# Attention and a mixture of experts on one core: joined normalisations, copies moved to ScalarE, and an earlier merge of the two output sums

## The reference, cut to what matters

```
x = x + xattn(layernorm(x), ctx, mask)      # x: 16 batches x 112 tokens x 512
x = x + ffn(layernorm(x), ...)

xattn:  scores = q @ m.T / sqrt(512), masked; softmax over 375; readout = attn @ m
ffn:    probs = softmax(x @ gate.T)            # 1792 tokens, 64 experts
        top 8 of each token, weights normalised to sum 1
        experts that are only second choices (rank 5 to 8 of every token that has them) and are
        similar enough to a first choice are replaced by it
        y = down_e(silu(gate_e(x)) * up_e(x))   # 192 inner columns
        out[token] += weight * y
layernorm(x) = (x - mean) / sqrt(var + 1e-5)    # no scale, no shift
```

## Time and profile before

| | |
|---|---|
| median of three runs | 810.89 us |
| profiled execution | 809.93 us, its span 808.1 us |
| PE, busy share of the span | 84% |
| DVE | 69% |
| POOL | 64% |
| ACT | 56% |
| mean granted clock of TensorE | 0.934 of full speed |
| memory traffic | 190 MB, mean 235 GB/s |

### The profile page before, as it was taken

One profiled execution on the slowest core, in us unless ns is written; L12 is line 12 of the kernel. 1 busy time (PEld: TensorE's weight loads), 2 busy tenths in 40 slices (PEclk: granted clock), 3 DMA queues, 4 the chain that ended last, 5 costly groups with the idle time before them and its releaser, 6 DMA issues. The chain is left out here.

```text
span 808.1 us, 15268 instructions
## 1 busy us (share of the span) xinstructions
PE 678.4 (84%) x4278; PEld 560.5 (69%) x4278; DVE 554.3 (69%) x1308; ACT 453.6 (56%) x885; POOL 518.3 (64%) x461
## 2 busy tenths in 40 slices
PE   4999999731599999999999998989898998999730
PEld 2555555420489999888988888878787887888630
DVE  5699999962277666777677677676767776767620
ACT  3544554210266666666775766767666676666620
POOL 6037777776638887887766666676657666666440
PEclk9999999955599999999999999999999999999965
DMA  8999896605659999999999999999999999999467
GB/s 281 373 369 336 292 312 232 206 18 161 171 153 221 241 234 242 237 239 257 244 270 254 272 243 245 258 234 260 241 252 222 252 236 240 237 248 242 92 124 159
DMA packets 107557, 189.93 MB, mean 235 GB/s; under 512 B 33521, under 2 KB 35441, under 8 KB 106065
## 3 DMA queue, kind: packets, MB, share of 16 engines
q1 hardware_dynamic: 74274, 125.61, 50.7%
q0 software_dynamic: 33200, 63.35, 38.1%
HBM read 143.40 MB, written 56.24 MB: 247 GB/s over the span
## 5 line engine op out<-in xcount | busy, mean ns | idle before, releaser
L1224 PE MATMUL bank<-xh,w1h 128*128 128x256 f32 (+7 forms) x768 | 228.8, 298 | 18.3 <-DVE h L897 18.2
L1226 PE MATMUL bank<-xh,w1l 128*128 128x256 f32 (+7 forms) x768 | 220.4, 287 | 0.0
L1225 PE MATMUL bank<-xl,w1h 128*128 128x256 f32 (+7 forms) x768 | 220.4, 287 | 0.0
L610 POOL DMA_INDIRECT xg<-normed_tokens,list x145 | 158.2, 1091 | 54.1 <-issue 48.2
L1224 PEld LDWEIGHTS bank<-xh,w1h 128*128 128x128 f32 x768 | 147.2, 192 | 23.4 <-issue 23.2
L619 POOL DMA_INDIRECT out_rows<-ys,list x73 | 115.8, 1587 | 70.9 <-ACT ys L1041 58.1
L594 POOL DMA_INDIRECT list_table<-token,slot x112 | 114.4, 1022 | 69.8 <-DVE token L765 36.6
L619 POOL DMA_INDIRECT second_sum<-ys,list x70 | 113.3, 1618 | 66.4 <-ACT ys L1041 45.5
L913 DVE TENSOR_TENSOR xl<-bank,xh 128x448 fp32r<-128x448 f32 (+3 forms) x145 | 84.2, 616 | 97.3 <-ACT xh L1048 96.3
L1225 PEld LDWEIGHTS bank<-xl,w1h 128*128 128x128 f32 x768 | 147.7, 192 | 0.0
L1226 PEld LDWEIGHTS bank<-xh,w1l 128*128 128x128 f32 x768 | 147.5, 192 | 0.0
(11 more groups left out here) (210 smaller groups left out, 1104.4 us busy)
## 6 DMA issues: line engine op xcount, KB each, us to landing
raw<-in_w SPq DMA_DIRECT2D x195, 256.0 KB, 4.7
raw<-in_w2a SPq DMA_DIRECT2D x65, 256.0 KB, 4.5
ctxT_s<-in_ctxT SPq DMA_DIRECT2D x16, 768.0 KB, 8.4
ctx_s<-in_ctx SPq DMA_DIRECT2D x16, 768.0 KB, 8.1
raw<-in_w2b SPq DMA_DIRECT2D x65, 128.0 KB, 5.8
list_table<-blank SPq DMA_DIRECT2D x30, 256.0 KB, 6.7
x_in<-in_x SPq DMA_DIRECT2D x16, 224.0 KB, 7.9
out_rows<-x SPq DMA_DIRECT2D x16, 224.0 KB, 6.6
```

The lines of the kernel that those rows point to most:

```text
L610: pool.indirect_dma_start(xg[u.on(XGS)][0:u.m, t, :], None, normed, bass.IndirectOffsetOnAxis(ap=lists[u.on(LISTS)][0:u.m, t, 0:1], axis=0 ...
L1224: pe.matmul(bank[m][:, 0:W], wh, mh, start=(c == 0), stop=False)
L1225: pe.matmul(bank[m][:, 0:W], wh, ml, start=False, stop=False)
L1226: mm = pe.matmul(bank[m][:, 0:W], wl, mh, start=False, stop=(c == DK - 1))
```

## The change

1. The two normalisations share their tiles, two columns wide, and one chain `scales(s)` on VectorE: column 0 is the x of batch s+1, column 1 the x1 of batch s-2. Statistics of x are made one slot earlier (lag -2), x is loaded one slot earlier (lag -4), and the pipeline has one more slot in front, -4, that only loads. `newton` works on two columns at once.
2. `publish` moves to ScalarE, at the end of its slot; VectorE keeps the counting of token numbers (`count_tokens`), with a semaphore of its own, `c_token`, for which POOL waits as well.
3. The merge is issued before the late loop, when all static scatters have landed; `scatter_over` waits for it and adds to `out`.

```diff
         def phase1(eng, body):
-            for n in range(-3, B + 5):
+            for n in range(-4, B + 5):
                 body(At(n))
...
-                batches(s, (-3, load_x), (-2, load_ctxT), (-1, load_ctx))
+                batches(s, (-4, load_x), (-2, load_ctxT), (-1, load_ctx))
...
+                split_wait(pool, c_token, (b.n + 1) * TOKEN)
                 split_wait(pool, c_slots, (b.n + 1) * SLOTS)
...
                 split_wait(pool, ys_s, u.t0 + 1)
-                pool.indirect_dma_start(second, bass.IndirectOffsetOnAxis(ap=over_list[:], axis=0),
+                pool.wait_ge(merged, 16)
+                pool.indirect_dma_start(out, bass.IndirectOffsetOnAxis(ap=over_list[:], axis=0),
...
+            for i in range(2):
+                pool.wait_ge(scattered[i], SUM_TILES[i] * 16)
+            pool.dma_start(out[0:TOK, :], second[0:TOK, :], accum_op=ALU.add, max_dma_last_dim=8192).then_inc(merged, 16)
             overs = overs_of(pool)
             with pool.Fori(0, overs) as g:
                 keep_list(Unit(STATIC, g))
                 gather(Unit(STATIC, g + 1))
                 scatter_over(Unit(STATIC, g))
-            pool.wait_ge(scattered[0], SUM_TILES[0] * 16)
-            split_wait(pool, scattered[1], (overs + SUM_TILES[1]) * 16)
-            pool.dma_start(out[0:TOK, :], second[0:TOK, :], accum_op=ALU.add, max_dma_last_dim=8192).then_inc(merged, 16)
...
+            def scales(s):
+                if not -1 <= s.n < B + 2:
+                    return
+                ch = Chain(dve, c_scale, SCALED, s.n + 1)
+                dve.wait_ge(c_norm, min(s.n + 2, B) * NORM)
+                wait(dve, c_resid, min(max(s.n - 1, 0), B) * RESID)
+                yield from ch.link(v.tensor_scalar(rstd["var"][:], mv[s.n % 2][:, :, 1], EPS, None, ALU.add), tell=True)
+                dve.wait_ge(rough_s, (s.n + 2) * 2)
+                yield from ch.link(v.tensor_tensor(rstd["square"][:], rstd["rough"][:], rstd["rough"][:], ALU.mult))
+                yield from ch.link(v.scalar_tensor_tensor(rstd["half"][:], rstd["square"][:], -0.5, rstd["var"][:], ALU.mult, ALU.mult))
+                wait(dve, xn_s, min(s.n + 1, B))
+                wait(dve, xn2_s, min(max(s.n - 2, 0), B))
+                yield from ch.link(v.scalar_tensor_tensor(rstd["exact"][:], rstd["half"][:], 1.5, rstd["rough"][:], ALU.add, ALU.mult))
+                yield from ch.link(v.scalar_tensor_tensor(rstd["shift"][:], mv[s.n % 2][:, :, 0], -1.0, rstd["exact"][:], ALU.mult, ALU.mult), tell=True)
+                ch.done()
...
-                yield from ch.link(v.tensor_scalar(slot8[b.four][:], bank[7][:, 0:ENTERS], -1.0, float(PAD_LIST), ALU.mult, ALU.add))
-                yield from ch.link(v.tensor_copy(token[b.four][:, :, 1].bitcast(F32), bank[7][:, ENTERS:2 * ENTERS]))
                 yield from ch.link(v.tensor_scalar(token[b.four][:, :, 0], token[b.four][:, :, 0], 4 * T, None, ALU.add), tell=True)
...
-                    taking_turns(s, (4, place_entries), (3, top), (-1, norm_and_scale), (2, renormed_x))
+                    going = [scales(s)]
+                    batches(s, (4, lambda b: going.append(place_entries(b))), (3, lambda b: going.append(top(b))),
+                            (-2, lambda b: going.append(norm(b))))
+                    turns(*going)
                 taking_turns(s, (0, score))
                 if s.n == 0:
                     constants()
                 taking_turns(s, (1, resid))
-                taking_turns(s, (4, publish))
+                taking_turns(s, (4, count_tokens))
...
+            for i in range(2):
+                v.memset(mv[i][:], 1.0).then_inc(primed, 1)
+            dve.wait_ge(primed, 2)
             phase1(dve, slot)
...
+            def rough(s):
+                if -1 <= s.n < B + 2:
+                    act.wait_ge(c_scale, (s.n + 1) * SCALED + 1)
+                    a.activation(rstd["log"][:], rstd["var"][:], ACT.Ln).then_inc(rough_s, 1)
+                    act.wait_ge(rough_s, (s.n + 1) * 2 + 1)
+                    a.activation(rstd["rough"][:], rstd["log"][:], ACT.Exp, scale=-0.5).then_inc(rough_s, 1)
+            def publish(b):
+                act.wait_ge(spread_ps, b.n + 1)
+                wait(act, tabled[b.four], b.turn4 * ENTERS * 16)
+                a.activation(slot8[b.four][:], bank[7][:, 0:ENTERS], ACT.Copy, scale=-1.0, bias=float(PAD_LIST))
+                a.copy(token[b.four][:, :, 1].bitcast(F32), bank[7][:, ENTERS:2 * ENTERS]).then_inc(c_slots, SLOTS)
...
-            phase1(act, lambda s: batches(s, (1, copy_pT), (-1, rough(rough_a, c_norm, NORM, rstd_a)), (2, norm_x1),
-                                          (3, exps), (-1, norm_x), (2, copy_xn2T), (0, exp_scores), (-1, copy_xnT),
-                                          (1, rough(rough_c, c_resid, RESID, rstd_c))))
+            def slot(s):
+                batches(s, (1, copy_pT))
+                rough(s)
+                batches(s, (2, norm_x1), (3, exps), (-1, norm_x), (2, copy_xn2T), (0, exp_scores), (-1, copy_xnT), (4, publish))
```

More of the change, by code:

```diff
@@ L164, in two1 @@
             return [sb1(f"{name}{i}", shape, dt) for i in range(2)]
-        def rstd_tiles(name):
-            return {k: early.enter_context(nc.sbuf_tensor(f"rstd_{name}_{k}", [T, 1], F32)) for k in ("var", "log", "rough", "square", "half", "exact")}
         def sem(name):
@@ L239, in program @@
         mask_s = sb1("mask_s", [B, M], U8); masked = sb1("masked", [B, M], BF16); of_batch = sb1("of_batch", [B, B, T], BF16)
-        st_a = sb1("st_a", [T, 6]); mv_a = sb1("mv_a", [T, 2]); rstd_a = rstd_tiles("a")
+        st_a = sb1("st_a", [T, 6]); mv = two1("mv", [T, 2, 2])
+        rstd = {k: sb1(f"rstd_{k}", [T, 2]) for k in ("var", "log", "rough", "square", "half", "exact", "shift")}
         xn = two1("xn", [T, D])
         xnT = two1("xnT", [P, DK, T])
-        shift_a = sb1("shift_a", [T, 1]); shift_c = sb1("shift_c", [T, 1])
         nmax = two1("nmax", [T, 1])
@@ L249, in program @@
         rinv = sb1("rinv", [T, 1]); rval = sb1("rval", [T, 1])
-        st_c = sb1("st_c", [T, 6]); mv_c = sb1("mv_c", [T, 2]); rstd_c = rstd_tiles("c")
+        st_c = sb1("st_c", [T, 6])
         xn2T = two1("xn2T", [P, DK, T])
@@ L660, in norm @@
                 dve.wait_ge(x_in[b.on(XS)], (b.nth(XS) + 1) * 16)
-                wait(dve, xn_s, b.n)
                 yield from ch.link(v.bn_stats(st_a[:], xa[b.on(XS)][:]))
-                yield from ch.link(v.bn_aggr(mv_a[:], st_a[:]))
-                yield from ch.link(v.tensor_scalar(rstd_a["var"][:], mv_a[:, 1:2], EPS, None, ALU.add), tell=True)
+                yield from ch.link(v.bn_aggr(mv[(b.n + 1) % 2][:, 0, :], st_a[:]), tell=True)
                 ch.done()
[L667 to L671, removed]
@@ L678, in normed_x @@
                 ch.done()
-            def norm_and_scale(b):
-                yield from norm(b)
-                yield from normed_x(b)
             def score(b):
@@ L704, in resid @@
                 yield from ch.link(v.bn_stats(st_c[:], x1[b.on(STORED)][:]))
-                yield from ch.link(v.bn_aggr(mv_c[:], st_c[:]))
-                yield from ch.link(v.tensor_scalar(rstd_c["var"][:], mv_c[:, 1:2], EPS, None, ALU.add), tell=True)
-                ch.done()
-            def renormed_x(b):
-                ch = Chain(dve, c_renorm, RENORM, b.n)
-                dve.wait_ge(rough_c, (b.n + 1) * 2)
-                wait(dve, xn2_s, b.n)
-                yield from newton(ch, rstd_c)
-                yield from ch.link(v.tensor_scalar(shift_c[:], mv_c[:, 0:1], -1.0, rstd_c["exact"][:], ALU.mult, ALU.mult), tell=True)
+                yield from ch.link(v.bn_aggr(mv[b.n % 2][:, 1, :], st_c[:]), tell=True)
                 ch.done()
@@ L996, in copy_xnT @@
                 a.activation(xnT[b.par][:], bank[0][:, 0:DK * T].rearrange("p (c t) -> p c t", c=DK), ACT.Copy, scale=SCALE).then_inc(xnT_sb, 1)
-            def rough(s, c, links, r):
-                def stage(b):
-                    act.wait_ge(c, (b.n + 1) * links)
-                    a.activation(r["log"][:], r["var"][:], ACT.Ln).then_inc(s, 1)
-                    act.wait_ge(s, b.n * 2 + 1)
-                    a.activation(r["rough"][:], r["log"][:], ACT.Exp, scale=-0.5).then_inc(s, 1)
-                return stage
+            def rough(s):
[9 more added lines that the diff above has]
+                a.copy(token[b.four][:, :, 1].bitcast(F32), bank[7][:, ENTERS:2 * ENTERS]).then_inc(c_slots, SLOTS)
             nc.scalar.preload_act_table_set("natural_log_exp_and_others")
```

25 lines of the change are left out of this document (10 added, 15 removed).

## The result

The changed kernel takes 805.14 us (median of 5 runs, 803.35 to 807.05), the kernel before beside it 812.53 us (median of 5 runs, the three known before among them): ratio 0.9924, 95% interval 0.9899 to 0.9949. (The ratio on record isn't the quotient of these two medians, which would be 0.9909.) In a second measurement it gave 0.994 (0.9928 to 0.9952), 805.5 against 810.88 us, while a copy of the kernel before gave 1.0013 (0.9997 to 1.0029). It is faster by 0.6 to 0.8%, some 5 to 6 us. I had forecast 812.3 us and a range down to 808.0: wrong in sign and outside the range.

What follows compares the result with a forecast made beforehand. POOL's 112 list scatters were taken to bound routing, and one chain through the merge the end. Routing +0.2 and merge +1.2 us on the median 810.89 gave 812.3 us, range 808.0 to 815.0.

Steps and rivals of the forecast that it cites:

- Start and first token: Ahead of the first list scatter: start +0.4 us, ScalarE's publish -0.2 us, PE's waits unchanged; routing together +0.2 us.
- rival 4: Routing stage: PE and ScalarE wait on the joined root, POOL starves and loses 3 us, 815 us in all; chance 0.13.
- Take 0; bounds -3 and +3: Routing stage: list scatters lengthened beside VectorE's products, 5.8 us in all, stay as they are since the same products stay.
- rival 3: Routing stage: freed VectorE shortens it, -9 us (some 803); small form, collisions halved, -3 us (809); chance 0.10.
- So 796.2 + 3.7 + 0.6 = 800.5: End: merge's landing alone at 796.2, plus 3.7 us for loads and 0.6 for the gather inside it; end +1.2 us.
- rival 1: End: loads slip into the merge's gaps and cost it little; tail -3.1 us, 808.0 in all; chance 0.20.
- Rival 2: End: the speculative unit's gather stands behind the merge on q0 and its chain ends the program, +2 to +3 us; chance 0.15.
- Sum: Whole kernel: routing +0.2 and merge +1.2 us give +1.4 us, so 812.3 us on the scale of the medians.

Runs made afterwards that it cites:

- a_again: The changed kernel measured once more, unchanged, against the kernel before: ratio 0.994, 805.5 against 810.88 us.
- after_wait: The changed kernel with one more wait on GpSimd, already satisfied, ahead of the late scatter: 841.44 us, a single run.
- gather_late: The changed kernel with the late loop's gather issued behind the late scatter instead of ahead of it: ratio 0.9981 to the kernel before.
- weights_late: The changed kernel with SyncE's late weight loads held back until the merge has landed: ratio 0.996 to the kernel before, against 0.9934 without the hold.
- keep_first: The changed kernel with the first keep_list ahead of the merge and the next list's copies behind the late scatter: ratio 0.9996 to the kernel before, 810.4 us.

## Why the prediction was wrong

**Start and first token.** Held: the spread 0.26 us later, ScalarE's copies 0.33 us quicker, first scatter within 0.1 us of before. VectorE now waits for the joined root (4.2 us over 13 slots) without starving POOL: rival 4 did not come.

**"Take 0; bounds -3 and +3" for the collisions.** This is the first step that failed, a term put at nothing. The row shortened by 2.0 us in this trace, 2.7 on the mean of two traces of each kernel (147.6 to 144.9): 1.0 us by the pace, which no step of mine had, and 1.7 by fewer lengthened scatters and pauses, which is rival 3's small form. I had the whole of the lengthening at 5.8 us, and took the middle of the bounds because the same products stay. They do, but the scatters that took over 1.0 us went from 15 and 15 to 13 and 12. Joined and publish alone both gain, which supports the direction, but why the edit shortened the row and didn't lengthen it is argued from the phase and not shown.

The Trainium skill (SBUF — State Buffer, "SBUF: two separate sides") states that a VectorE instruction with two SBUF inputs and a GpSimd instruction that reads SBUF exclude each other from a shared pair of ports for a whole instruction. The traces agree in where the lengthened scatters lie, beside VectorE's products (0.68 us each). Of the sign of the change the rule says nothing, as the products stay.

**"So 796.2 + 3.7 + 0.6 = 800.5."** This is the second step that failed, of about the same size, and a term that was mis-sized. Measured from the last static scatter's issue, the merge should have landed after 4.8 + 24.5 = 29.3 us; it landed after 4.4 + 22.3 = 26.7, and in six more traces, a_again to after_wait, it took 21.7 to 22.0 (22.2 in gather_late). The end shortened from 37.4 us on the mean of the eight traces with the merge behind (36.9 to 37.9) to 36.0 on that of the seven with it ahead and the loop's order kept (35.8 to 36.4): -1.4 us instead of +1.2. The sum put the end at 36.9 + 1.2 = 38.1 us, 2.1 more than the 36.0: the merge went out 0.4 sooner and took 21.9 on the mean, 2.6 less, while a wait of 0.8 us between its landing and the late scatter's issue (26.3 to 27.1) stood nowhere in the sum. The other 0.5 is luck of the trace that I started from, the shortest end of its eight. I priced each load at its share of all 16 engines, on the reading that a share of 0.95 is a full pipe. The windows of the two merges show that it is not. Before, the merge alone (length of the stretch, busy us and counts of PE, PEld, DVE, ACT, POOL, clock, DMA share, GB/s):

```profile
789.00:794.00 5.00, 0.00 (x0) 0.00 (x0) 0.00 (x0) 0.00 (x0) 0.00 (x0) 0.50 1.05 216
794.00:799.00 5.00, 0.00 (x0) 0.00 (x0) 0.00 (x0) 0.00 (x0) 0.00 (x0) 0.50 1.04 216
```

After, with the loads inside:

```profile
780.00:785.00 5.00, 0.00 (x0) 0.00 (x0) 0.00 (x0) 0.00 (x0) 0.00 (x0) 0.50 1.04 208
785.00:790.00 5.00, 0.00 (x0) 0.00 (x0) 0.00 (x0) 0.00 (x0) 1.12 (x1) 0.50 1.02 229
790.00:795.00 5.00, 0.00 (x0) 0.00 (x0) 0.00 (x0) 0.00 (x0) 0.00 (x0) 0.50 0.98 248
```

At a share no higher than before the engines moved up to 248 GB/s instead of 216. So the share told that packets were in flight all the time, and not how many bytes could still pass. And the DMA queues of after from 777 to 795.6 us (packets, MB, share) against the earlier trace rows:

```profile
q0 software_dynamic: 496, 3.28, 85.9%
q1 hardware_dynamic: 686, 1.01, 16.1%
```

The loads' 1.01 MB took 16.1% of 18.6 us = 3.0 us of all engines, close to my 3.7, while the merge paid 1.1 to 1.3 of it (the difference that weights_late took away). That is rival 1, for about two thirds of the price. The other part of the margin is order: the list takes 10.2 us in the merge, so the gather goes out late, lands with the merge and costs it little: with the list and the gather alone beside it the merge takes 20.5 to 20.7 us, against 20.0 to 20.4 with nothing.

**Rival 2** has its place as described, but not the point from which it decides, "later than the merge by over 0.5 us". In the changed kernel the gather lands 0.7 us behind the merge (796.28 against 795.6) and costs nothing, since VectorE's end at 801.23 has 4.1 us to the end of the span; in gather_late it lands 5.9 us behind the merge (839.91 against 834.05) and sets the end. I had compared VectorE's end with the late scatter's landing and left out what POOL still does behind that landing. The price of the order in POOL's stream was the larger one, as keep_first shows, 5.1 us, and no rival had it.

**Sum.** The two traces of each kernel differ by 3.4 us (808.1 and 808.1 to 805.3 and 804.2): +0.3 first scatter, -2.7 row, 0 expert loop, -1.0 end (37.2 to 36.2). The times differ by 5 to 6 by the ratios. Both profiled executions of the kernel before lie under the medians of their runs (809.93 against 810.89 or 812.53, and 809.92 against 810.57), both of the changed kernel above theirs (807.05 against 805.14, 805.98 against 805.5); the remaining 2 us or so are in runs without a profile and can't be placed.

## What to carry to other kernels

A DMA share near 1.0 during a memory-to-memory transfer need not be a full pipe (216 GB/s at 1.05 here, and 248 at 0.98): compare GB/s with other stretches before charging every transfer put beside it in full, and ask which of the transfers pays. The work that ended last isn't always what the end waits for: look at how far the end of the span lies behind it in other kernels, 0.2 us in one here and 4.1 in another. In a serial end, the order of issue on one engine and one queue (what stands 1 us behind a long transfer, what is left to do behind the last landing) was worth more (5 us) than the transfer's own shift (3 us at best). Where an engine's row sets a stage, count what lengthens its instructions, not only what fills its gaps: taking 0.4 us of small work per slot off another engine came with a gain of up to 3 us here.

## What the runs showed of the hardware

- The merge, 3584 KB adding from memory to memory, takes 20.0 to 20.4 us alone, 20.5 to 20.7 with only a list's load and a gather beside it, 21.7 to 22.3 with 1.15 MB of loads (22.2 with these and no gather), and 24.5 with a gather issued 1.4 us behind it on its own queue.
- A load of 8 KB put into it took 10.2 us; loads of 128 and 256 KB about 17 us.
- The step between two indirect scatters on GpSimd differed by 9 ns between programs, constant within each.
- The routing stage's row takes 144 to 148 us on some chips and 170 to 176 on others; the changed kernel had 144.4 and 145.3 on the first kind and 175.0 on the second.
